# Rounding of the quantised weights on VectorE in fourteen pieces ahead of the output addition of attention 1

## The reference, cut to what matters

```python
x = x + attention0(layernorm(x), ctx, Wq, Wkv, Wout)           # 16 heads of 16, softmax
x = x + ffn0(layernorm(x), clip_x, clip_down, w_gate, w_up, w_down)
x = x + mlstm_attention(layernorm(x), ctx, ctx, ...)           # 4 heads
x = x + mixture_of_experts(layernorm(x), gate_w, w1, w3, w2)   # 8 experts, top 2

def ffn0(x, clip_x, clip_down, w_gate, w_up, w_down):
    xq = act_fake_quant(x, clip_x)
    h = act_fake_quant(silu(xq @ q(w_gate).T) * (xq @ q(w_up).T), clip_down)
    return h @ q(w_down).T
def q(w):                       # _weight_fake_quant, one scale per row
    scale = max(|w|, axis=1) / 127
    return clip(round(w / scale), -128, 127) * scale
```

## Time and profile before

| | |
|---|---|
| median of 3 runs | 858.18 us (857.07 to 863.29) |
| the profiled execution, its own time | 865.73 us |
| its span | 864.0 us |
| PE busy | 679.8 us (79%) |
| DVE busy | 527.0 us (61%) |
| ACT busy | 410.6 us (48%) |
| POOL busy | 278.8 us (32%) |
| mean granted clock of TensorE | 0.879 |

### The profile page before, as it was taken

The page is one execution under the profiler, slowest core; times in us unless marked ns, Lnnn a source line. Parts: engine busy times, 40 slices in busy tenths (PEclk is TensorE's granted clock), DMA queues, the critical chain, the costliest instruction groups (busy, mean ns, idle before and its releaser), DMA issues.

```text
span 864.0 us, 19336 instructions
## 1 busy us (share of the span) xinstructions
PE 679.8 (79%) x4571; PEld 471.9 (55%) x4615; DVE 527.0 (61%) x1371; ACT 410.6 (48%) x831; POOL 278.8 (32%) x390
## 2 busy tenths in 40 slices
PE   2999999885853991577417989898989998989992
PEld 2788887663322670466404556565656555655661
DVE  5577789985867452788785464646454555464441
ACT  1466655556874463345225444545353545553430
POOL 3111111111436001644302263535354253553421
PEclk9799999986978795555558999999999999999996
DMA  8100000000000114211270514243331525431213
GB/s 260 32 13 12 16 14 13 0 1 1 0 0 12 44 42 159 87 28 27 97 245 19 169 30 132 67 128 73 105 90 31 170 34 165 124 73 24 34 22 110
DMA packets 45844, 58.41 MB, mean 68 GB/s; under 512 B 13497, under 2 KB 39417, under 8 KB 45273
## 3 DMA queue, kind: packets, MB, share of 16 engines
q1 hardware_dynamic: 38328, 47.79, 16.9%
q0 software_dynamic: 7488, 10.31, 7.2%
HBM read 145.90 MB, written 11.80 MB: 183 GB/s over the span
## 4 chain that ended last, share of the span: by engine, by line
PE 48%; DVE 18%; issue 14%; POOL 7%; DMA 3%; ACT 3%; DVEq 2%; POOLq 1%; ACTq 1%; SPq 0%
PE psum L995 16%; PE psum L1017 7%; PE psum L718 3%; PE psum L1008 3%; POOL region L658 3%; PE psum L702 3%; PE psum L725 3%; PE psum L895 2%; PE psum L738 1%; PE psum L757 1%; PE psum L707 1%; PE psum L840 1%; PE psum L888 1%; DVE region L1358 1%; DMA region<-xrow_dram,next_token 1%
## 5 line engine op out<-in xcount | busy, mean ns | idle before, releaser
L995 PE MATMUL psum<-region 128*128 x897 | 209.6, 382 | 19.8 <-POOL pause_p L660 6.2
L995 PEld LDWEIGHTS psum<-region 128*128 128x128 bf16 x936 | 91.6, 98 | 119.1 <-issue 30.4
L1017 PE MATMUL psum<-region 128*128 x936 | 112.5, 278 | 6.2 <-DVE region L1868 3.7
L1017 PEld LDWEIGHTS psum<-region 128*128 128x128 bf16 x936 | 91.3, 100 | 22.3 <-issue 9.2
L1261 ACT ACTIVATE region<-psum 128x512 f32<-128x512 f32 x78 | 46.5, 596 | 115.0 <-PE psum L995 104.2
L1838 DVE TENSOR_TENSOR region<-psum,region 128x512 f32<-128x512 f32 x78 | 53.9, 690 | 72.9 <-ACT region L1261 62.9
L628 POOL TENSOR_TENSOR pause_p<-minus_half 128x1 f32<-128x1 f32 x37 | 7.1, 193 | 191.4 <-DVE next_token L1854 190.6
L640 POOL DMA_INDIRECT sum_dram<-region,tok_idx x39 | 62.0, 1589 | 6.6 <-issue 6.3
L1282 ACT ACTIVATE pause_a<-one_col 128x1 f32<-128x1 f32 x117 | 23.7, 202 | 84.1 <-issue 70.2
L525 POOL TENSOR_TENSOR region<-region,pair_mask 128x256 f32<-128x256 f32 x32 | 18.9, 612 | 137.8 <-ACT region L1062 137.8
L1868 DVE TENSOR_TENSOR region<-psum,region 128x1024 bf16<-128x1024 f32 x39 | 47.6, 1222 | 20.1 <-ACT region L1269 20.1
(11 more groups left out here) (304 smaller groups left out, 1386.0 us busy)
## 6 DMA issues: line engine op xcount, KB each, us to landing
region<-in_L_ffn_w SPq DMA_DIRECT2D x117, 1024.0 KB
region<-in_ctx SPq DMA_DIRECT2D x48, 128.0 KB, 2.1
region<-neg_max_dram SPq DMA_DIRECT2D x4, 1024.0 KB, 7.6
xrow_dram<-region SPq DMA_DIRECT2D x1, 2080.0 KB, 7.8
x_sb<-in_x SPq DMA_DIRECT2D x4, 512.0 KB, 7.1
sum_dram<-x_sb SPq DMA_DIRECT2D x1, 2048.0 KB, 7.5
region<-in_L_ffn_w_down SPq DMA_DIRECT2D x1, 704.0 KB, 8.1
region<-in_L_ffn_w_gate SPq DMA_DIRECT2D x1, 640.0 KB, 8.6
```

The costliest lines, as they stand in the source:

```text
L995: last = mm(psum[:, 2 * f + n, :], (xT_lo if xl else xT_hi)[:, p, k, :], weights_at(place, wl, n, k * F1 + f * FH, FH), start=(i == 0), st ...
L1017: last = mm(psum[:, 7, 0:D], (hT_lo if hl else hT_hi)[:, f, :], weights_at(place, wl, 2, f * D, D), start=(i == 0), stop=(i == 3 * (F1 // ...
```

## The change

VectorE's loop over steps is written out. The weights' work is cut into pieces that are given to steps 2 to 15 as lists, and `step` runs its list between `softmax_shift(b, 1)` and `tail_add(b - 1)`, no longer behind `tail_add`. The normalisation of x1 goes in lots of 8, 4 and 4 batches, with the first eight and next four in steps 12, 13 and 15. GpSimd's loop over `mask_k` is written out too, with the power of the first lot after `mask_k(12)`, that of the second after `mask_k(15)`. PE, ScalarE and SyncE keep their instructions and order.

```diff
+    THIRDS = (slice(0, B // 2), slice(B // 2, EARLY), slice(EARLY, B))
@@ GpSimd
-            mask_k(0, 0)
-            mask_k(1, 1)
-            with pool.Fori(0, (B - 2) // 2) as i:
-                mask_k(2 * i + 2, 0, inner=True)
-                mask_k(2 * i + 3, 1, inner=True)
-            for n, part in enumerate((slice(0, EARLY), slice(EARLY, B))):
+            def x1_rstd(n):
+                part = THIRDS[n]
                 pool.wait_ge(ln2_eps, n + 1)
                 nc.gpsimd.tensor_tensor(rstd[:, part], rstd[:, part], minus_half[:, part], ALU.pow).then_inc(rstd2_ready, 1)
+            for b in range(B):
+                mask_k(b, b % 2)
+                if b == EARLY:
+                    x1_rstd(0)
+            x1_rstd(1)
+            x1_rstd(2)
@@ VectorE
                 softmax_shift(b, 1)
+                for work in late:
+                    work()
                 if inner or b >= 1:
                     tail_add(b - 1)
-                if late:
-                    late()
...
+                part = slice(n * 2 * IT // 3, (n + 1) * 2 * IT // 3)
+                nc.vector.tensor_reduce(w_amax[:, part], wgu[:, part, :], AX.X, ALU.max, apply_absolute_value=True)
...
+            def gate_up_shifted(n):
+                part = wgu[:, n * IT:(n + 1) * IT, :]
...
             step(0, 0)
-            rest = (gate_up_maxima, weight_scales, down_rounded, gate_up_scaled, gate_up_shifted, gate_up_rounded, early_norms)
...
+            late[2] = [lambda: gate_up_maxima(0)]
+            late[3] = [lambda: gate_up_maxima(1)]
+            late[4] = [lambda: gate_up_maxima(2)]
+            late[5] = [down_maxima]
+            late[6] = [weight_scales, lambda: down_scaled_up(0)]
+            late[7] = [lambda: down_scaled_up(1), down_shifted]
+            late[8] = [down_rounded, lambda: gate_up_scaled(0, 1)]
+            late[9] = [lambda: gate_up_scaled(1, 5)]
+            late[10] = [lambda: gate_up_scaled(5, 8), lambda: x1_eps(0)]
+            late[11] = [lambda: gate_up_scaled(8, 12)]
+            late[12] = [lambda: gate_up_shifted(0), lambda: early_norms(0, 0, 2)]
+            late[13] = [lambda: gate_up_shifted(1), lambda: early_norms(0, 2, 4)]
+            late[14] = [lambda: x1_eps(1), gate_up_rounded]
+            late[15] = [lambda: early_norms(0, 4, 8), lambda: early_norms(1, B // 2, EARLY)]
+            for b in range(1, B):
+                step(b, b % 2, late=late[b])
```

More of the change, by code:

```diff
@@ L1388, in token_stats, with step @@
                 nc.vector.tensor_copy(mv[:, b, :], mv1[:]).then_inc(chain, 1)
-            def step(b, p, inner=False, late=None):
+            def step(b, p, inner=False, late=()):
                 softmax_shift(b, 0)
@@ L1410, in link, with gate_up_maxima, down_maxima, gate_up_scaled @@
                 dve.wait_ge(b_chain, counted[0])
-            def gate_up_maxima():
-                dve.wait_ge(fw_loaded, 112)
-                dve.wait_ge(fw_preset, 6)
-                nc.vector.tensor_reduce(w_amax[:, 0:2 * IT], wgu, AX.X, ALU.max, apply_absolute_value=True)
+            def gate_up_maxima(n):
+                if n == 0:
+                    dve.wait_ge(fw_loaded, 112)
+                    dve.wait_ge(fw_preset, 6)
+                part = slice(n * 2 * IT // 3, (n + 1) * 2 * IT // 3)
+                nc.vector.tensor_reduce(w_amax[:, part], wgu[:, part, :], AX.X, ALU.max, apply_absolute_value=True)
+            def down_maxima():
+                link(nc.vector.tensor_reduce(w_amax[:, 2 * IT:2 * IT + KT], wd, AX.X, ALU.max, apply_absolute_value=True))
             def weight_scales():
-                link(nc.vector.tensor_reduce(w_amax[:, 2 * IT:2 * IT + KT], wd, AX.X, ALU.max, apply_absolute_value=True))
                 link(nc.vector.tensor_scalar_mul(w_scale[:], w_amax[:], 1.0 / QMAX))
                 link(nc.vector.reciprocal(w_inv[:], w_scale[:]))
-            def gate_up_scaled():
-                for n in range(2 * IT):
+            def gate_up_scaled(first, end):
+                for n in range(first, end):
                     last = nc.vector.tensor_scalar(wgu[:, n, :], wgu[:, n, :], w_inv[:, n:n + 1], QMAX, ALU.mult, ALU.min)
-                link(last)
-            def gate_up_shifted():
-                link(nc.vector.tensor_scalar(wgu, wgu, -QMAX - 1.0, MAGIC, ALU.max, ALU.add))
+                if end == 2 * IT:
+                    link(last)
+            def gate_up_shifted(n):
+                part = wgu[:, n * IT:(n + 1) * IT, :]
+                last = nc.vector.tensor_scalar(part, part, -QMAX - 1.0, MAGIC, ALU.max, ALU.add)
+                if n == 1:
+                    link(last)
             def gate_up_rounded():
@@ L1449, in norm_x1, with early_norms @@
                                             ALU.subtract, ALU.mult).then_inc(x1n_step, 1)
-            def early_norms():
-                dve.wait_ge(rstd2_ready, 1)
-                norm_x1(range(EARLY))
+            def early_norms(n, first, end):
+                if first == THIRDS[n].start:
+                    dve.wait_ge(rstd2_ready, n + 1)
+                norm_x1(range(first, end))
             step(0, 0)
-            rest = (gate_up_maxima, weight_scales, down_rounded, gate_up_scaled, gate_up_shifted, gate_up_rounded, early_norms)
-            with dve.Fori(0, (B - 1 - len(rest)) // 2) as i:
-                step(2 * i + 1, 1, inner=True)
-                step(2 * i + 2, 0, inner=True)
-            for b in range(B - len(rest), B):
-                step(b, b % 2, late=rest[b - (B - len(rest))])
+            late = [[] for b in range(B)]
+            late[2] = [lambda: gate_up_maxima(0)]
[14 more added lines that the diff above has]
+                step(b, b % 2, late=late[b])
             tail_norm(B - 1)
@@ L1466, in _ @@
             dve.wait_ge(ln2_chain, 3 * B)
-            nc.vector.tensor_scalar_add(rstd[:, EARLY:B], mv[:, EARLY:B, 1], LN_EPS).then_inc(ln2_eps, 1)
+            x1_eps(2)
             dve.wait_ge(clip_exp, 1)
@@ L1474, in _ @@
             link(nc.vector.tensor_tensor(x1_range[:], x1_range[:], mv[:, :, 0].unsqueeze(1).to_broadcast([P, 2, B]), ALU.subtract))
-            dve.wait_ge(rstd2_ready, 2)
+            dve.wait_ge(rstd2_ready, 3)
             link(nc.vector.tensor_tensor(x1_range[:], x1_range[:], rstd[:].unsqueeze(1).to_broadcast([P, 2, B]), ALU.mult))
```

18 lines of the change are left out of this document (11 added, 7 removed).

## The result

| | before | after |
|---|---|---|
| median of 20 runs each | 859.96 us (856.33 to 863.29) | 852.18 us (849.11 to 858.15) |
| ratio after / before | | 0.9915 (95% interval 0.9900 to 0.9931) |
| span of the profiled execution | 864.0 us | 850.5 us |
| mean granted clock | 0.879 | 0.889 |
| attention 1, first maxima of step 1 to its last operation on VectorE | 164.99 us | 157.21 us |

The change brings 7.8 us, 0.85% (0.7 to 1.0%), within the 1% that had got a chance of 0.74. The forecast of 852.3 us lies on the measured median, but by luck, through two errors that cancel: the gain is 7.8 and not 5.9, and the median of before, over twenty runs, is 859.96 and not 858.18.

The account below looks back on a forecast made before the run. PE was taken to bound attention 1, with VectorE's extra work fitting a hole ahead of the addition. Terms 7.35 - 2.6 + 1.2 gave 5.95, so 5.9 us off the 858.18 median: 852.3 us, range 848.5 to 856.0.

Parts of the forecast that it names:

- the 1% that had got a chance of 0.74: Whole kernel: a measured time within about 1% of before, 849.6 to 866.8 us, chance 0.74.
- What bounds the kernel: Attention 1 runs at PE's pace, 9.93 us a step; VectorE has about 1.85 us of room ahead of the addition.
- These six lose 7.35 us: Steps 9 to 14 of before take 66.93 us against 59.58, since extra work stands behind the addition.
- The hold by the masks: From step 6, GpSimd's masks and VectorE's `tensor_scalar` exclude each other: 0.73 us a list, 2.6 us lost together.
- Rival 1 (no hold): Lists from step 6: masks add only 0.13 us, gain 8.05 us, 850.1 us; chance 0.22.
- Rival 2 (the power holds VectorE): Step 11: GpSimd's power also holds VectorE's scalings, over by 1.6 us, gain 4.3, 853.9 us; chance 0.15.
- Rivals 3 and 4: Steps 6 to 13, more holds or critical additions: no gain, 858 us, 0.10; steps 1 to 8, code fetching: 867 us, 0.03.
- Step 15: PE's idle 2.58 us shrinks to about 0.9, clock may stay high, 0.39 wait goes; gain 0.4 to 1.4, taken 1.2.
- its sign: Step 15: PE's idle before L753 at about 1 us and a granted clock of 1.00 behind it.
- The sum: Whole kernel: 7.35 - 2.6 + 1.2 = 5.95 us gain, subtracted as 5.9 from the median of 858.18.

Follow-up runs that it names:

- e4: The changed kernel plus unused work: maxima in steps 2 and 4, a GpSimd power in step 7, a GpSimd multiplication in step 9; 853.73 us, one execution.
- e2: The changed kernel with its fourteen lists of small pieces put back behind `tail_add`; 854.0 us, ratio 0.9943 to the kernel before.
- e1: The kernel before with its whole, uncut pieces moved ahead of the output addition; 861.42 us, ratio 1.0038 to the kernel before.
- e3: The changed kernel with GpSimd's masks laying out only 8 of 128 tokens from batch 2 on, part of the computation left out; 851.91 us, one execution.
- e5: The kernel before with only step 14's rounding of gate and up and preparation of the first lot moved ahead of the addition; 855.90 us, one execution.
- e6: The changed kernel with lists evened out: begun one step earlier, shift and rounding in thirds, seven normalisations in step 15; 849.8 us, ratio 0.9891 to before.
- r_e1: A second profile of the kernel before with whole pieces moved ahead of the addition, nothing else changed; 866.36 us, one execution.

## Why the prediction was right, and where not

**What bounds the kernel: right.** Steps are at PE's pace, the hole ahead of the addition is real, and a list inside it costs nothing: steps 2 to 6 took 9.93 to 9.98, e4's 2.86 as well. The room was forecast as 1.85 and is 1.80.

**"These six lose 7.35 us": right in sum, too simple in its reason.** After, they lose 1.03. But the prediction let each microsecond behind the addition be paid beyond 0.3. By e2 a lag is carried from step to step, and 3.0 of the gain in the steps comes from the smaller lists and not from the place; a reader who took over only the rule "ahead of the addition" would get e1, which is slower than before.

**The hold by the masks: right mechanism, wrong size.** This is the term that was mis-sized. It was put at 0.73 a list, one wait of 0.13 and a whole mask of 0.6 between two operations. It is at most 0.44 (1.01 against 0.57 in e3). The timeline of GpSimd in the kernel after shows the turns, in steps 7, 8, 11, 12 and 14:

```profile
100.59 1.19 POOL L526 TENSOR_TENSOR region<-region,pair_mask 128x256 f32<-128x256 f32 x2 [8.76 <-ACT region L1064]
...
110.77 1.91 POOL L526 TENSOR_TENSOR region<-region,pair_mask 128x256 f32<-128x256 f32 x2 [9.00 <-ACT region L1064]
...
141.76 1.68 POOL L539 TENSOR_TENSOR rstd<-rstd,minus_half 128x8 f32<-128x8 f32 x1
...
150.55 1.98 POOL L526 TENSOR_TENSOR region<-region,pair_mask 128x256 f32<-128x256 f32 x2 [7.10 <-ACT region L1064]
...
171.68 2.52 POOL L539 TENSOR_TENSOR rstd<-rstd,minus_half 128x4 f32<-128x4 f32 x1
```

In step 7 the masks keep their length (1.19) and VectorE's first scaling waits for both. In steps 8 and 12 VectorE's first operation goes in between, the masks take 1.91 and 1.98, and VectorE's second is the one that waits: 1.03 for two normalisations in step 12 in place of the 0.73 of e3. Either way VectorE waits once and not twice, 0.44 in the first case and 0.18 to 0.35 in the second; a single long operation in between, as in e5, does not wait at all. Step by step, over 9.93:

| step | 6 | 7 | 12 | 13 | 14 | sum |
|---|---|---|---|---|---|---|
| forecast | 0.1 | 0.5 | 0.4 | 0.5 | 1.1 | 2.6 |
| measured | 0.0 | 0.25 | 0.09 | 0.02 | 0.89 | 1.25 |

With 0.03 in steps 10 and 11 it is 1.28, and the gain is larger by 1.3. In steps 12 and 13 the smaller hold brings the addition to 2.96, at the edge of the room; by the line above, 0.3 more would have cost 0.3.

**Rival 1 (no hold)** has a gain of 8.05, nearer to the 7.8 than the prediction's own case, but its reason does not stand: the hold is there. **Rival 2 (the power holds VectorE)** has fallen. In the kernel after, the power of 8 columns starts at 141.76 and takes the forecast 1.6 (1.68), and the four scalings beside it take 1.56, the same as in step 9, where there is none; step 11 takes 9.94:

```profile
121.30 1.56 DVE L1430 TENSOR_SCALAR region<-region,w_inv 128x256 f32<-128x256 f32 x4
...
141.18 1.56 DVE L1430 TENSOR_SCALAR region<-region,w_inv 128x256 f32<-128x256 f32 x4
```

The Trainium skill, SBUF — State Buffer, section "Who interferes with whom", lets the exclusion last for the whole instruction on either side. The masks and e4's multiplication agree with it in kind, though VectorE waits somewhat less than they last (0.44 where 0.63 of the masks was left, 0.79 for the 1.09 of the multiplication); the power does not, and e4's of 3.18 us is the plainest case. **Rivals 3 and 4** are out: the gain is there, and steps 1 to 6 of the written-out loop are as long as the looped ones.

**Step 15: what was forecast came, but one step of the reason is wrong, and the size too small.** PE's idle time shrank and the clock stayed up, as forecast. The timeline of PE in the kernel after shows its waits of 0.8 us and more:

```profile
174.33 0.65 PE L740 MATMUL psum<-region 128*32 128x128 f32 x16 [0.82 <-DVE x_sb L1374]
...
179.24 0.44 PE L753 MATMUL psum<-ident,region 128*128 128x128 f32 x2 [0.98 <-DVE region L1369]
...
182.72 1.09 PE L727 MATMUL psum<-ident,region 128*128 128x128 f32 x8 [1.05 <-ACT region L1068]
184.63 1.08 PE L740 MATMUL psum<-region 128*32 128x128 f32 x32 [0.81 <-DVE x_sb L1374]
...
188.25 0.39 PE L753 MATMUL psum<-ident,region 128*128 128x128 f32 x2
```

0.98 is what was forecast as about 1. The gain is 1.72 and not 1.2, so beyond the upper end of 1.4 that the text gave for it. Of that forecast 0.4 was the wait of PE behind the normalisations; it is gone here (the last row has no bracket), but e5 keeps the normalisations behind the addition and ends as early. And e2, with PE idle for 2.42 us and the clock at 1.00, ends as early too. So the whole 1.72 belongs to the clock. The prediction let the clock's fall follow from the stall of 2.58, and it made that stall's end its sign; e2 shows that a stall nearly as long need not bring the clock down, and e3 that idle times of a microsecond do not save it.

**The sum.** 7.35 - 1.28 + 1.72 = 7.8, against 7.35 - 2.6 + 1.2 = 5.95. The median taken for before was 1.8 too low, which three runs between 857.07 and 863.29 could not tell. That the forecast hit the median is luck: from the right median it would have read 854.0.

**What stays open.** What brings the clock down: e3, with the idle times of the kernel after, lost it in both of its profiles, and e2, with nearly that of before, kept it. And what decides which operation goes first when GpSimd's two masks and a list meet. The distance alone does not: in the kernel after the list starts 0.56 or 0.57 us behind the masks in all of steps 7 to 13. The lists of steps 7, 9, 10 and 11 begin with a scaling by `w_inv`, and there both masks go first; those of steps 8, 12 and 13 begin with a shift or a rounding by constants, and these go in between. e6 divides in the same way at the same distance. But in steps 11, 12 and 14 of e1 and step 14 of e5, where the list starts 0.46 or 0.47 behind the masks, the first operation goes in between whichever it is. No run varied distance or operation by itself.

## What to carry to other kernels

Find the hole of the engine that has time to spare (here 1.80 us on VectorE, between its last necessary operation and the one that PE's product releases), and cut the extra work so that each piece fits, the hold by the other engine included; whole pieces in the right place were slower than in the wrong one, since they made PE stand and some of the stalls brought the clock down. Work behind the critical operation is not paid once a step, since a lag is carried: measure the growth of it. And price a stall of PE, where PE bounds, with the clock that it may cost, 1.2 to 4.3 us here, more often than not more than the stall. But read the clock of each profile before putting the time down to the stall.

## What the runs showed of the hardware that was not expected

- A GpSimd power runs beside a VectorE `tensor_scalar` without slowing it (3.18 us beside 1.00), but not the other way: the power of 4 columns in step 14 takes 2.52 us beside the rounding, and 1.01 by itself. It began 0.52 behind the rounding's start and ended 0.86 behind the rounding's end. In e2 and e3 it is 2.45 beside a rounding of 1.75, with no full mask near, and ends 0.88 and 0.87 behind it. Beside the four short scalings of step 11 a power of 8 columns is hardly longer, 1.68 with a forecast of 1.64.
- A pair of masks, 1.19 us long, costs a VectorE list of `tensor_scalar` 0.43 or 0.44 us where both masks go first, 0.18 to 0.35 where VectorE's first operation goes in between, and nothing where that is the whole list (1.76, e5); a following multiplication of 1.09 us costs it 0.79.
- The granted clock fell to 0.50 behind PE's idle time of 1.77 us in e1, of 1.39 and 1.60 us in r_e1 (for some 10 us in e1, 7 and 10 in r_e1, 2.3 to 4.3 us lost each time); behind 2.11 us in both; behind 2.6 us in both executions of before; and behind 0.8 to 1.05 us in e3 alone. It stayed at 1.00 behind 2.42 us in e2, and behind 1.39 and 1.60 us in e1.
